# Expert stages of a two-layer metaformer: first product computed already transposed, from fp32 weights loaded per block

## The reference, cut to what matters

```
# layer 0: D = 128, FF = 512
h = silu(xt @ W1[e]) @ W2[e]                    # per expert e
# layer 1: F = 256, and the kernel holds w1 and w3 side by side as 512 columns
h = (silu(x @ w1[e]) * (x @ w3[e])) @ w2[e]
```

## Time and profile before

| what | value |
|---|---|
| median of three timed runs | 1649.24 us |
| span of the profiled execution | 1726.5 us |
| mean granted TensorE clock in it | 0.833 |
| PE busy | 1207.4 us (70%) |
| DVE busy | 1106.1 us (64%) |
| POOL busy | 699.3 us (41%) |
| ACT busy | 587.5 us (34%) |
| moved by DMA | 129.26 MB |
| most moved in one of the page's 40 slices | 273 GB/s |

### The profile page before, as it was taken

One profiled execution on the slowest core, in us unless ns is written; L12 is line 12 of the kernel. 1 busy time (PEld: TensorE's weight loads), 2 busy tenths in 40 slices (PEclk: granted clock), 3 DMA queues, 4 the chain that ended last, 5 costly groups with the idle time before them and its releaser, 6 DMA issues. The chain is left out here.

```text
span 1726.5 us, 31708 instructions
## 1 busy us (share of the span) xinstructions
PE 1207.4 (70%) x6568; PEld 956.4 (55%) x6569; DVE 1106.1 (64%) x4125; ACT 587.5 (34%) x1099; POOL 699.3 (41%) x680
## 2 busy tenths in 40 slices
PE   4799903223222999999946979889797089999940
PEld 4799902212122999998934545455454067777730
DVE  7677704434345666666648688787876467777754
ACT  4233303323231444444432234334344134444320
POOL 0100005565574444444434045345554535555530
PEclk9899955555555999999976989989898589999975
DMA  4033297121111222222232011121011122222239
GB/s 200 22 107 106 64 121 273 53 58 55 39 44 46 66 62 62 62 63 60 62 128 79 1 46 51 28 58 42 26 32 31 40 73 74 75 79 71 73 103 261
DMA packets 139200, 129.26 MB, mean 75 GB/s; under 512 B 56291, under 2 KB 119012, under 8 KB 138214
## 3 DMA queue, kind: packets, MB, share of 16 engines
q1 hardware_dynamic: 89396, 79.76, 16.9%
q0 software_dynamic: 19968, 39.44, 7.0%
q10 hardware_dynamic: 29778, 9.45, 2.7%
HBM read 78.66 MB, written 50.99 MB: 75 GB/s over the span
## 5 line engine op out<-in xcount | busy, mean ns | idle before, releaser
L594 POOL DMA_INDIRECT routed<-r_xn,r_slot x320 | 333.3, 1042 | 346.6 <-DVEq L583 233.9
L823 POOL DMA_INDIRECT answers<-e_y,e_dest x304 | 291.1, 958 | 347.1 <-ACT e_y L922 272.9
L972 DVE COPY e_ht<-e_ps_ht 128x512 f32<-128x512 f32 (+1 forms) x304 | 169.5, 558 | 180.9 <-PE e_ps_ht L859 156.7
L867 PE MATMUL e_ps_y<-w,e_ht 128*128 x1824 | 258.6, 278 | 13.4 <-DVE e_ht L972 7.4
L867 PEld LDWEIGHTS e_ps_y<-w,e_ht 128*128 128x128 f32 x1824 | 228.6, 192 | 20.1 <-issue 18.8
L1135 PE MATMUL c_pz<-c_c,down 116*120 116x512 f32 (+1 forms) x392 | 199.7, 627 | 0.0
L922 ACT ACTIVATE e_y<-e_ps_y,e_weight 128x128 f32<-128x128 f32 x304 | 111.8, 368 | 217.7 <-issue 117.9
L859 PE MATMUL e_ps_ht<-ident,e_h 128*128 128x128 f32 x912 | 150.8, 274 | 6.0 <-DVE e_h L958 5.5
L849 PE MATMUL e_ps_h<-w1h,e_xl 128*128 x308 | 150.9, 490 | 1.1 <-issue 0.7
L1109 PE MATMUL c_py<-c_xh,gl 121*116 121x512 f32 (+1 forms) x196 | 124.1, 633 | 39.1 <-DVE c_xl L1215 27.1
L859 PEld LDWEIGHTS e_ps_ht<-ident,e_h 128*128 128x128 f32 x912 | 115.4, 141 | 56.0 <-DVE e_h L958 10.7
(11 more groups left out here) (134 smaller groups left out, 2445.4 us busy)
## 6 DMA issues: line engine op xcount, KB each, us to landing
e_xg<-routed SPq DMA_DIRECT2D x318, 66.0 KB
answers<-answers SPq DMA_DIRECT2D x32, 480.0 KB
c_w<-in_w SPq DMA_DIRECT2D x32, 448.0 KB
c_x<-in_xh SPq DMA_DIRECT2D x4, 1536.0 KB
routed<-r_xn,r_slot POOLq DMA_INDIRECT x320
answers<-e_y,e_dest POOLq DMA_INDIRECT x304
x<-x SPq DMA_DIRECT2D x96, 48.0 KB
w1l<-in_w SPq DMA_DIRECT2D x2, 2048.0 KB, 10.3
```

The lines of the kernel that those rows point to most:

```text
L594: ro.nc.gpsimd.indirect_dma_start(ro.xs, bass.IndirectOffsetOnAxis(ap=ro.slot[0:px, q, c:c + 1], axis=0), ro.xn[0:px, q, k, t, :], None).t ...
L823: nc.gpsimd.indirect_dma_start(ys, bass.IndirectOffsetOnAxis(ap=dest[:, s:s + 1], axis=0), y[:, s, :], None).then_inc(stored[s], 16)
L867: ins = nc.tensor.matmul(ps_y[s % 2][:, 0:P], ht[:, s % 2, c * P:(c + 1) * P], wt.w2[:, bass.ds(w + c * P, P)], start=c == 0, stop=c == ch ...
L972: nc.vector.tensor_copy(ht[:, s % 2, :], ps_ht[s % 2][:, 0:HID]).then_inc(ht_ready, 1)
```

## The change

The first product is turned round. The weights become the stationary operand, 128 hidden columns at a time, and the transposed tokens move: `ps_h` then holds hidden values on partitions, which is the form that the second product needs. So `turn_h`, the copy to `ht` and the PSUM tiles between them go; silu (or the gate product) writes `ht` itself. The product is plain fp32, so that the splits into high and low parts go too, of the tokens and of the weights. The first weights no longer stay in SBUF: SP loads the 256 KB of the block's expert for every block into a ring of four slots (`w1s`), three blocks ahead. For this the table has a third row with the block's expert, and the first weights have another order in DRAM (expert first).

PE's step becomes `first_product(b + 2)`, `turn_x(b + 4)`, `second_product(b)`, with one read of packed experts at the start of each turn.

```diff
-        self.w1h, self.w1l, self.w2 = sb("w1h", F32R), sb("w1l", F32R), sb("w2")
+        self.w2 = ctx.enter_context(nc.sbuf_tensor(f"w2_{layer}", [P, EXPERTS * self.chunks * P], F32))
 ...
-    eng.dma_start(wt.w1f, io[f"w1_{layer}"].rearrange("p e f -> p (e f)")).then_inc(w_in, 16)
...
+    ch.after(nc.vector.tensor_copy(r.table[:, 2, :], t_e[:]))
...
-            act.wait_ge(w_in, 32)
-            nc.scalar.activation(wt.w1h[:], wt.w1f, ACT.Copy).then_inc(w_split, 1)
...
-            dve.wait_ge(w_split, 1)
-            nc.vector.tensor_tensor(wt.w1l[:], wt.w1f, wt.w1h[:].bitcast(F32), ALU.subtract)
...
+        WSLOTS, WAHEAD = 4, 3
+        xg, w1s = sb("xg", [P, U, PAY]), sb("w1", [P, WSLOTS, FF])
-        xh, xl = sb("xh", [P, 2, P], F32R), sb("xl", [P, 2, P], F32R)
-        h, ht, y = sb("h", [P, 2, HID]), sb("ht", [P, 2, HID]), sb("y", [P, U, P])
-        ps_x, ps_h, ps_ht, ps_y = ps("x"), ps("h"), ps("ht"), ps("y")
+        xt, ht, y = sb("xt", [P, 2, P]), sb("ht", [P, 2, HID]), sb("y", [P, U, P])
+        ps_x, ps_h, ps_y = ps("x"), ps("h"), ps("y")
...
         @block.sync
+            expert = lambda b: sp.value_load(r.table[0:1, 2, bass.ds(b, 1)], min_val=0, max_val=EXPERTS - 1)
             def load(b, slot, again):
                 start = row(b)
                 if again:
-                    sp.wait_ge(x_split, b - U + 1)
+                    sp.wait_ge(x_copied, b - U + 1)
                 sp.dma_start(xg[:, slot, :], xs[bass.ds(start, P), :]).then_inc(x_in[slot], 16)
+            def load_weights(b, slot, again):
+                e = expert(b)
+                if again:
+                    sp.wait_ge(h_ready, b - WSLOTS + 1)
+                sp.dma_start(w1s[:, slot, :], w1[bass.ds(e, 1)].rearrange("e p f -> p (e f)")).then_inc(w1_in[slot], 16)
-            for s in range(AHEAD):
+            for s in range(WAHEAD):
                 load(s, s, False)
+                load_weights(s, s, False)
+            for s in range(WAHEAD, AHEAD):
+                load(s, s, False)
             def step(it, s, first):
                 b = U * it + s
+                load_weights(b + WAHEAD, (s + WAHEAD) % WSLOTS, not first or s + WAHEAD >= WSLOTS)
                 load(b + AHEAD, (s + AHEAD) % U, not first or s + AHEAD >= U)
...
-                nc.tensor.matmul(ps_h[i][:], xl[:, i, :], wt.w1h[:, bass.ds(w, FF)], start=True, stop=False)
-                nc.tensor.matmul(ps_h[i][:], xh[:, i, :], wt.w1l[:, bass.ds(w, FF)], start=False, stop=False)
-                nc.tensor.matmul(ps_h[i][:], xh[:, i, :], wt.w1h[:, bass.ds(w, FF)], start=False, stop=True
+                pe.wait_ge(x_copied, b + 1)
+                pe.wait_ge(w1_in[slot], 16 * (w_turn + 1))
+                if not early:
+                    pe.wait_ge(ht_ready, b - 1)
+                for c in range(FF // P):
+                    ins = nc.tensor.matmul(ps_h[i][:, c * P:(c + 1) * P], w1s[:, slot, c * P:(c + 1) * P], xt[:, i, :],
+                                           start=True, stop=True)
+                ins.then_inc(h_ready, 1)
...
-                for c in range(chunks):
-                    ins = nc.tensor.transpose(ps_ht[s % 2][:, c * P:(c + 1) * P], h[:, s % 2, c * P:(c + 1) * P], r.ident[:])
...
+                if s == 0:
+                    w[:] = weights_of(b)
+                first_product(b + 2, s + 2, TURNS * it + (s + 2) // WSLOTS, False)
+                turn_x(b + 4, s + 4, it + (s + 4) // U, False)
+                second_product(b, s, w[s], first and s < 2)
...
-                    nc.scalar.activation(h[:, i, :], ps_h[i][:], ACT.Silu).then_inc(hid_ready, 1)
+                        act.wait_ge(y_done, b - 1)
+                    nc.scalar.activation(ht[:, i, :], ps_h[i][:], ACT.Silu).then_inc(ht_ready, 1)
...
-                nc.vector.tensor_copy(xh[:, i, :], ps_x[i][:, 0:P]).then_inc(hi_done, 1)
-                dve.wait_ge(hi_done, b + 1)
-                nc.vector.tensor_tensor(xl[:, i, :], ps_x[i][:, 0:P], xh[:, i, :].bitcast(F32), ALU.subtract
-                                        ).then_inc(x_split, 1)
+                nc.vector.tensor_copy(xt[:, i, :], ps_x[i][:, 0:P]).then_inc(x_copied, 1)
...
-                nc.vector.tensor_tensor(h[:, i, :], gate[:, i, :], ps_h[i][:, HID:2 * HID], ALU.mult
-                                        ).then_inc(hid_ready, 1)
+                nc.vector.tensor_tensor(ht[:, i, :], gate[:, i, :], ps_h[i][:, HID:2 * HID], ALU.mult
+                                        ).then_inc(ht_ready, 1)
...
-                nc.vector.tensor_copy(ht[:, s % 2, :], ps_ht[s % 2][:, 0:HID]).then_inc(ht_ready, 1)
...
-    io["w1_0"] = np.asarray(a["L0_ffn_W1"]).transpose(1, 0, 2)
+    io["w1_0"] = np.asarray(a["L0_ffn_W1"])
```

More of the change, by code:

```diff
@@ L364, in __init__ @@
         self.wg = sb("wg", [P, 2, EXPERTS])
-        self.table = sb("table", [1, 2, TABLE], I32)
+        self.table = sb("table", [1, 3, TABLE], I32)
         self.gh = sb("gh", [P, N_UP * PPX], F32R)
@@ L761, in _, with expert_phase @@
             nc.vector.tensor_tensor(r.gl[:], fa[:], r.gh[:].bitcast(F32), ALU.subtract)
[L762 to L768 removed]
+def expert_phase(nc, r, wt, layer, xs, ys, w1):
+    chunks = wt.chunks
     HID = chunks * P
@@ L815, in _ @@
                 sp.wait_ge(x_in[s], 16 * (STEPS + (1 if s < AHEAD else 0)))
+            for s in range(WSLOTS):
+                sp.wait_ge(w1_in[s], 16 * (U // WSLOTS * STEPS + (1 if s < WAHEAD else 0)))
         @block.gpsimd
@@ L830, in _, with weights_of @@
         def _(pe):
-            def experts_from(b):
-                return pe.value_load(r.table[0:1, 1, bass.ds(b, 1)], min_val=0, max_val=EXPERTS ** 8 - 1)
-            def weights_of(experts, n):
-                return ((experts >> (3 * n)) & (EXPERTS - 1)) * FF
+            def weights_of(b):
+                experts = pe.value_load(r.table[0:1, 1, bass.ds(b, 1)], min_val=0, max_val=EXPERTS ** 8 - 1)
+                return [((experts >> (3 * n)) & (EXPERTS - 1)) * HID for n in range(U)]
             def turn_x(b, s, turn_no, early):
@@ L929, in step, with copy_x @@
                 b = U * it + s
-                if not (first and s == 0):
-                    answer(b - 1, s - 1)
+                answer(b, s)
                 activate(b + 2, s + 2, False)
             steps(act, step)
-            answer(BLOCKS - 1, U - 1)
         @block.vector
         def _(dve):
-            def split(b, s, turn_no, early):
+            def copy_x(b, s, turn_no, early):
                 dve.wait_ge(x_turned, b + 1)
@@ L955, in gate_product @@
                 if not early:
[L956 removed]
+                    dve.wait_ge(y_done, b - 1)
                 i = s % 2
[L958 to L965 removed]
+                nc.vector.tensor_tensor(ht[:, i, :], gate[:, i, :], ps_h[i][:, HID:2 * HID], ALU.mult
+                                        ).then_inc(ht_ready, 1)
+            copy_x(0, 0, 0, True)
+            copy_x(1, 1, 0, True)
+            for b in range(2, 4):
+                if layer:
+                    gate_product(b - 2, b - 2, True)
+                copy_x(b, b, 0, False)
             def step(it, s, first):
                 b = U * it + s
[L969 to L972 removed]
                 if layer:
[L974 to L975 removed]
+                    gate_product(b + 2, s + 2, False)
+                copy_x(b + 4, s + 4, it + (s + 4) // U, False)
             steps(dve, step)
[L977 to L978 removed]
 class Answers:
```

95 lines of the change are left out of this document (26 added, 69 removed).

## The result

| what | before | after |
|---|---|---|
| median, same chip | 1648.05 us (1646.61 to 1649.58) | 1813.12 us (1810.55 to 1813.68) |
| ratio | | 1.101, 95% interval 1.099 to 1.103 |
| span of the profiled execution | 1726.5, first profile; 1641.7, on a chip of about this speed | 1811.9 us |
| granted clock, mean | 0.833 and 0.850 | 0.858 |
| moved by DMA | 129.26 MB | 206.35 MB |

A forecast was written before the change was run, and what follows sets the result against it. PE was taken to bound layer 0 and no single engine layer 1, with SP the bound after the change. Expert stages +57 and +110, stage ends -8, gave +159, scaled to +152 on 1649: 1801 us, range 1705 to 1885.

The forecast's parts named there:

- SP as bound: Both expert stages: SP's two table reads and issues set the pace, 2.54 us a block, +167 us together.
- The price of an issue: One read-and-issue on SP: 1.27 us in the loop, 1.10 unrolled, bounded by 1.10 and 1.36.
- The end of a stage: Each expert stage: last used weights issued 7 issues (8.9 us) before SP's end at 394, POOL's last issue at 392.
- PE: Expert stages: 17 passes, 1.89 us a block in layer 0; 13 passes, 1.44 us in layer 1.
- The loop through answer and silu: Layer 1's second product through answer and silu: nothing under SP's slower pace, otherwise up to 0.1 to 0.2 us a block.
- Stage ends: POOL's scatters ahead of the expert stages: without the weights' low part on DVE, 4.4 and 3.6 us back, -8.
- The base: Whole kernel: timed runs are 4.5% shorter than the 1726.5 us span, so +159 is scaled by 0.955 to 152.
- A: Faster: outside the profiler an SP issue costs less than 0.9 us, PE sets the pace; -63 us, 1586; chance 0.08.
- B: Much slower: PE's clock is low for half of layer 0's blocks; +81 us, 1882; chance 0.10.
- C: Much slower: SP's table read stretches to 0.60 us, an issue costs 0.33 more; +198 us, 1999; chance 0.02.
- D: Late transfers: the weights' DMA reaches only twice 61 GB/s, 3.2 us a block; +192 us, 1993; chance 0.02.
- E: Near the turning point: SP issues cost 0.98 to 1.10 us; 0 to +75 us; chance 0.05.

The follow-up runs named there:

- e2: The changed kernel with a quarter of the first weights' bytes loaded, in the same number of issues: 1896.62 us, ratio 1.091 to the kernel before.
- e4: The kernel before with a second table read, wait and load of x per block into an unread buffer: 1869.34 us, ratio 1.075.
- e3: The changed kernel with weights always from expert 0, without that table read and address arithmetic: 1737.01 us, ratio 0.996 to the kernel before.
- e6: The changed kernel with one packed table read and wait for both loads, and eight weight slots loaded 7 blocks ahead: 1744.15 us, ratio 1.014.
- e8: The changed kernel with all first weights resident in SBUF and copied into the ring by DVE: 1714.64 us, ratio 0.996 to the kernel before.
- e9: e8 with, in layer 1, ACT's silu before the answer and DVE's turned tokens first, gate product next, ring copy last: 1580.61 us, ratio 0.958.
- e10: e9 with four slots for ht in place of two: 1571.29 us, ratio 0.954 to the kernel before.
- e11: The changed kernel with e9's new order of silu and gate product in layer 1: 1814.58 us, ratio 1.100 to the kernel before.
- e12: The kernel before, unchanged, profiled once more on a chip of the faster kind: 1643.53 us.
- e5: The changed kernel, unmodified, on the chip that also ran e6 and e8: 1885.28 us, ratio 1.094 to the kernel before.
- e1: The kernel before, unchanged, profiled again on a slower chip: 1739.24 us.

## Why the prediction was right

**SP as bound: right, and the mechanism is shown.** Its main signs named in advance are there: alternation at 1.2 us without waits, equal stages, PE at its first products some 2.7 us after the issue. e2 rules the bytes out, and e4 makes most of the loss from an added issue alone. e3 takes it away by shortening the instruction string, and so does e6 (with its deeper ring); both keep the number of DMAs, so the number isn't it. e8 takes it away by removing the string.

**The price of an issue.** Forecast 1.27 us in the loop; measured (384.0 - 26 x 1.09) / 287 = 1.24, and 1.09 where unrolled (forecast 1.10). That is the middle of the bounds 1.10 and 1.36, so the lean to the loop's rows was a little too strong. The upper bound was too high, probably because of waits in it that the trace did not show as such; no run tests that. 0.03 x 287 is 9 us a stage, and the sum took 314 steps where first to last issue has 313, which is 1 more.

**The end of a stage: wrong in detail, and hidden.** I let the last weights used be issued 7 issues before the end. But PE's last step makes the first product of block 153, whose weights are issued three issues before the end (873.77 of 877.43), and POOL comes 2.5 us after SP's last issue, not 2 before. That is 4.5 us too short per stage; with the 10 too long the stage came out at 386.5 instead of 392. That the two errors have opposite signs is luck.

**PE.** 1.89 us a block in layer 0 is what e3, e8, e9 and e10 have (1.896); 1.44 in layer 1 is what e10 has (1.449). Both were right and neither mattered after the change.

**The loop through answer and silu.** At nothing under SP's cover: right (e11). Without cover 0.1 to 0.2 us a block: wrong, it was 1.98 - 1.44 = 0.54 (e8, from the 3.96 us of two blocks), because I took the lengths of the operations and not the order in which ACT and DVE reach them.

**Stage ends.** Forecast -8. What the low part did to POOL's scatters came as costed. At the end of layer 0's routing, first before (e12), then after:

```profile
450.78 7.37 POOL L594 DMA_INDIRECT routed<-r_xn,r_slot  x1 [0.30 <-issue]
...
452.87 4.41 DVE L763 TENSOR_TENSOR w1l<-w1l,w1h 128x4096 fp32r<-128x4096 f32 x1
```

```profile
451.30 3.38 POOL L591 DMA_INDIRECT routed<-r_xn,r_slot  x1 [0.30 <-issue]
...
451.97 1.83 DVE L758 TENSOR_TENSOR gl<-factor_a,gh 128x1624 fp32r<-128x1624 f32 x1
```

Each of these scatters ends 0.87 or 0.88 us after DVE's operation (458.15 and 457.28; 454.68 and 453.80). In layer 1 the scatter beside the low part took 4.23 us in e12 and 4.51 in the first profile. All four traces of kernels with the low part have both long ones (7.4 to 7.6 and 4.2 to 4.5); all ten without it have 3.4 to 4.0 us in layer 0 and nothing above 2.3 in layer 1. That is 4.0 and some 3.3 us back, as 4.4 and 3.6 were forecast. The length of the stages around them doesn't show it: -7.7 and -4.8 for e5 beside e1, with a chip 20 us faster in it, and -3.4 and +4.2 after beside e12, where the whole stretch between the stages is 4 us longer after although the work that remains is the same. That stretch took 477 and 485 us in e10 and e9, so it moves by more than this term. Why it does is open.

**The base.** The sum was +159 against the span and I scaled it with 0.955 to 152, taking the 77 us for an effect of the profiler on everything. That step was wrong: the stage that PE sets is 335 us on every chip (335.2, 335.2, 334.9), SP's pace hardly moves (1.23 and 1.24), and the difference lies in the stage ahead (547 to 497 us), between, and in layer 1. Unscaled, the forecast would have been 1808. The sum beside e12 is 51.5 + 118.3 + 0.4 = 170 us, against 165 between the medians; the chip of e12 is 2 to 5 us faster than the one of the medians (1645.68 and 1643.53 against 1648.05). Layer 0's loss was sized 6 us too large (57). Layer 1's was sized 8 us too small (110), from a stage 1 of 282 us that is 269 in e12, less the 5 us by which the stage after came out shorter.

**The rivals.** A: the price does not shrink outside the profiler; the plain runs of this kernel and of e4 are as slow as the profiled ones. B: the clock stayed at 1.00 in both windows above with PE busy 87% and 68%; it was at 0.50 only in the first 13 us of stage 0 and in 15 of the first 18 us of stage 1. C: the table reads take 272 ns at the median. The Trainium skill (DMA: Bandwidth & Descriptors, Latency and other measured facts) gives tensor_load a floor of about 600 ns; this read on SP stays well under it. D: 2.7 us to PE's start, three blocks of lead, and e2. E: the price lies above 1.10 on the mean.

## What to carry to other kernels

A queue that issues DMAs is an engine, though no busy time shows it: count its instructions per block, price one read-compute-wait-issue from a stretch without waits (here 1.1 to 1.24 us), and compare it with the block before adding a second one. If a load per block needs an address from a table, read the table once for all loads of the block, or fill the ring from SBUF with an engine that has time. When a bound is removed, read the order of each in-order engine next: here the reorderings of e9 took the ratio from 0.996 to 0.958, more than the product that the change was about had brought.

## What the hardware showed beyond that

- Chips differ by up to 6% in the same kernel: 1648, 1649 and 1646 us on some, 1723 and 1742 on others. Each chip was used for one set of runs, so the chip and its state at that time can't be told apart. Of the 96 us between the spans of e1 and e12, 57 lie ahead of expert stage 0, 17 between the stages, 21 in expert stage 1 and nothing in expert stage 0; in the changed kernel (e5 and after) the expert stages differ by 5 and 3 of 70 us. Between 300 and 480 us PE waited for DVE's sequencer ahead of the ranks (L557) 94.8 us in 8 waits in e1, up to 15.4 each, against 35 to 38 us in 15 or 16 waits on faster chips. The cause is open; nothing here tests it.
- An issue costs 0.333 us on SP for 66 KB and for 256 KB, and 0.35 from ACT.
- Where a POOL scatter met these long operations of DVE, it lasted until 0.8 to 0.9 us after their end: 7.37 us where 1.83 and 4.41 us of DVE followed each other (e12), 3.38 where only the 1.83 was left (after), and 0.92 beside neither.
- In e8, ACT's answer started some 0.8 us after the modelled end of its second product in every second block, but 0.04 us after it in the others. Whether the completion was late or the modelled end is wrong stays open.
